# A decoder layer on one core: how the rounded tokens and the rounded FFN rows are turned

## Time and profile before

| what | us |
|---|---|
| median of 3 runs | 1321.93 (1319.57 to 1323.46) |
| the profiled execution | 1327.34 |
| its span, first to last instruction | 1325.5 |
| PE busy in the span | 1158.6 (87%) |
| DVE busy | 1048.7 (79%) |
| POOL busy | 951.8 (72%) |
| ACT busy | 866.6 (65%) |

### The profile page before, as it was taken

One profiled execution on the slowest core, in us unless ns is written; L12 is line 12 of the kernel. 1 busy time (PEld: TensorE's weight loads), 2 busy tenths in 40 slices (PEclk: granted clock), 3 DMA queues, 4 the chain that ended last, 5 costly groups with the idle time before them and its releaser, 6 DMA issues. The chain is left out here.

```text
span 1325.5 us, 33417 instructions
## 1 busy us (share of the span) xinstructions
PE 1158.6 (87%) x10082; PEld 828.7 (63%) x10082; DVE 1048.7 (79%) x3192; ACT 866.6 (65%) x1789; POOL 951.8 (72%) x1016
## 2 busy tenths in 40 slices
PE   4779998979989799899776699999999999999985
PEld 3566676757767576677543456666666666666652
DVE  5478886878868788788658688888888889888872
ACT  3467776767767677677756356666666666666664
POOL 0166675756756666667674499999999999999982
PEclk9879999998999999999886699999999999999997
DMA  5244654553445544454537244433334444444400
GB/s 193 73 152 139 199 174 159 175 174 119 142 160 174 167 135 147 145 174 154 167 134 281 90 137 120 126 124 124 131 132 130 131 132 135 135 135 135 127 25 24
DMA packets 87840, 186.57 MB, mean 141 GB/s; under 512 B 12176, under 2 KB 28816, under 8 KB 87760
## 3 DMA queue, kind: packets, MB, share of 16 engines
q1 hardware_dynamic: 86896, 185.02, 43.9%
q10 hardware_dynamic: 864, 0.66, 0.2%
HBM read 105.86 MB, written 54.61 MB: 121 GB/s over the span
## 5 line engine op out<-in xcount | busy, mean ns | idle before, releaser
L608 ACT ACTIVATE prob<-masked,negmax 128x128 f32<-128x128 f32 (+1 forms) x512 | 205.8, 452 | 129.7 <-DVE negmax L741 128.7
L741 DVE CUSTOM_DVE_ANT_0 masked<-s_ps,mask_f 128x128 f32<-128x128 f32 (+1 forms) x512 | 161.2, 352 | 43.4 <-issue 30.7
L988 PE MATMUL y_ps<-kv,toep 128*128 128x288 f16 x640 | 184.7, 289 | 1.4 <-DVE prod L1324 1.4
L990 PE MATMUL y_ps<-kv,toep 128*128 128x288 f16 x640 | 184.5, 288 | 0.0
L989 PE MATMUL y_ps<-kv,toep 128*128 128x288 f16 x640 | 184.5, 288 | 0.0
L1044 PE MATMUL f_ps<-w1T,xiT 128*128 128x512 bf16 (+1 forms) x768 | 174.7, 364 | 0.9 <-ACT xiT L1165 0.7
L1223 POOL TENSOR_TENSOR tree<-prod 128x512 f32<-128x512 f32 x128 | 163.2, 1275 | 1.2 <-DVE prod L1324 1.2
L386 POOL TENSOR_TENSOR kv_s<-kv_f,kv_s 128x1152 f16<-128x1152 f32 x64 | 154.5, 2415 | 11.4 <-ACT kv_s L622 11.3
L1172 ACT ACTIVATE silu<-gate,sx 128x512 f32<-128x512 f32 (+1 forms) x96 | 66.0, 687 | 139.6 <-DVE gate L1378 139.6
L747 DVE TENSOR_TENSOR pT_lo<-t_ps,pT_hi 128x384 f16<-128x384 f32 x256 | 140.8, 550 | 17.0 <-ACT pT_hi L616 16.5
L616 ACT CAST pT_hi<-t_ps 128x384 f16<-128x384 f32 x256 | 122.0, 477 | 41.6 <-PE t_ps L510 39.5
(11 more groups left out here) (154 smaller groups left out, 3540.3 us busy)
## 6 DMA issues: line engine op xcount, KB each, us to landing
kv_pairs<-kv_s SPq DMA_DIRECT2D x64, 576.0 KB, 4.0
kv<-kv_pairs SPq DMA_DIRECT2D x32, 1152.0 KB, 8.1
c_in<-in_ctxr SPq DMA_DIRECT2D x64, 192.0 KB, 3.5
x_in<-in_x SPq DMA_DIRECT2D x16, 512.0 KB, 6.1
q_st<-q_hi SPq DMA_DIRECT2D x128, 64.0 KB, 2.0
k_st<-k_hi SPq DMA_DIRECT2D x128, 64.0 KB, 2.0
x_res<-in_x SPq DMA_DIRECT2D x16, 512.0 KB, 5.1
x_after_attention<-x_out SPq DMA_DIRECT2D x16, 512.0 KB, 3.3
```

Source lines behind the costliest of these rows:

```text
L608: ins = nc.scalar.activation(prob[h % 2][:, at:at + w], masked[h % 2][:, at:at + w], ACT.Exp, bias=negmax[:, h % 2, t:t + 1], scale=-1.0)
L741: ins = nc.vector.tensor_tensor_reduce(masked[h % 2][:, at:at + w], s_ps[h % 2][:, at:at + w], mask_f[:, S - w:S], -1.0, FAR, ALU.add, ALU ...
L988: nc.tensor.matmul(dst, toep[p][:, 0, taps], c[:, 0, m], start=mt == 0, stop=False)
L990: mm = nc.tensor.matmul(dst, toep[p][:, 1, taps], c[:, 0, m], start=False, stop=mt == lt)
```

## The change

The two turns are done by DMA. SP issues `dma_start_transpose` from SBUF to SBUF: one for the 128 x 512 tokens, three for the 128 x 1408 hidden rows (chunks of 512, 512 and 384 columns). The PE transposes, the PSUM tile b_ps and the two ACT copies go. In SP's order of a round, the three hidden transposes of head r-3 stand ahead of `load_conv`, and the token transpose of head r-1 stands last, behind the two stores of y_out. `xiT_done` and `hiT_done` now count DMA completions (16 each). The down projection takes its blocks in the order 0 to 10 where it took 8, 9, 10, 0 to 7, still as a group of three and a group of eight; its first group now waits for all three chunks.

```diff
+            def turn_hidden(h):
+                for c, (at, w) in enumerate(CH):
+                    counts = (h * 3 + c + 1, h)
+                    for count in counts:
+                        if not isinstance(count, int):
+                            sp.lower_val(count)
+                    alone(sp, started)
+                    sp.wait_ge(hi_done, counts[0])
+                    if c == 0:
+                        reached(sp, d_full, counts[1])
+                    sp.dma_start_transpose(hiT[:, at // P:(at + w) // P, :], hid_i[:, at:at + w]).then_inc(hiT_done, 16)
+            def turn_tokens(h):
+                counts = (h + 1, h * 6)
...
+                alone(sp, started)
+                sp.wait_ge(xi_done, counts[0])
+                reached(sp, f_full, counts[1])
+                sp.dma_start_transpose(xiT[:], x_i[:]).then_inc(xiT_done, 16)
             def body(r, p, loop=False):
+                if live(r - 3, loop):
+                    turn_hidden(r - 3)
                 if live(r + 1, loop):
                     load_conv(sp, r + 1, 1 - p)
...
                     sp.wait_ge(out_done, r - 2)
                     for half in range(2):
                         sp.dma_start(tokens(out, r - 3, half), y_out[half * 64:half * 64 + 64, :]).then_inc(out_stored, 16)
+                if live(r - 1, loop):
+                    turn_tokens(r - 1)
```

```diff
             def gate_up(h, c, sides=(0, 1)):
                 at, w = CH[c]
                 if c == 0 and sides[0] == 0:
-                    pe.wait_ge(xiT_done, h + 1)
+                    pe.wait_ge(xiT_done, 16 * (h + 1))
...
-                    if c == 0 and side == 1:
-                        reached(pe, hiT_done, h * 2 - 1)
...
             def project_down(h, part):
-                pe.wait_ge(hiT_done, h * 2 + part + 1)
...
                 if part == 0:
-
+                    pe.wait_ge(hiT_done, 48 * (h + 1))
```

More of the change, by code:

```diff
@@ L860, in mixer @@
         sem(n) for n in ("xc_done", "amax_done", "vmax_done", "vrec_done", "sx_done", "xmul_done", "xt_done", "xi_done"))
-    xi_full, xiT_done = sem("xi_full"), sem("xiT_done")
+    xiT_done = sem("xiT_done")
     f_full, gate_done, silu_done, up_done, hid_done = (sem(n) for n in ("f_full", "gate_done", "silu_done", "up_done", "hid_done"))
@@ L864, in mixer @@
         sem(n) for n in ("hmax3_done", "hmax_done", "sh_done", "shr_done", "shi_done"))
-    ht_done, hi_done, hi_full, hiT_done = sem("ht_done"), sem("hi_done"), sem("hi_full"), sem("hiT_done")
+    ht_done, hi_done, hiT_done = sem("ht_done"), sem("hi_done"), sem("hiT_done")
     d_full, down_done, out_done, out_stored = sem("d_full"), sem("down_done"), sem("out_done"), sem("out_stored")
@@ L936, in mixer @@
     a_ps = ps("a_ps", [P, 512], F32)
-    b_ps = ps("b_ps", [P, 1024], BF16)
-    TURN = [(f_ps[1][:].bitcast(BF16), 8, IT - 8), (b_ps[:], 0, 8)]
     def rounds(eng, body):
@@ L1010, in mixed @@
                 mm.then_inc(yt_full, 1)
[L1012 to L1032, removed]
             def gate_up(h, c, sides=(0, 1)):
@@ L1046, in gate_up @@
                     mm.then_inc(f_full, 1)
+            PARTS = ((0, 3), (3, IT - 3))
             def project_down(h, part):
-                pe.wait_ge(hiT_done, h * 2 + part + 1)
-                t0, n = TURN[part][1:]
+                t0, n = PARTS[part]
                 if part == 0:
+                    pe.wait_ge(hiT_done, 48 * (h + 1))
                     pe.wait_ge(x2_done, min(h + 3, NH) if isinstance(h, int) else h + 3)
@@ L1055, in project_down @@
                 for t in range(t0, t0 + n):
-                    mm = nc.tensor.matmul(a_ps[:], hiT[:, t, :], w2T[:, t, :], start=t == TURN[0][1], stop=t == 7)
+                    mm = nc.tensor.matmul(a_ps[:], hiT[:, t, :], w2T[:, t, :], start=t == 0, stop=t == IT - 1)
                 if part == 1:
@@ L1069, in body @@
                     conv(r, p, 1)
-                if down_live:
-                    hidden_turned(r - 3, 0)
-                    hidden_turned(r - 3, 1)
                 if live(r - 1, loop):
@@ L1091, in body @@
                     conv(r, p, 3, (0,))
-                if live(r - 1, loop):
-                    tokens_turned(r - 1)
                 if conv_live:
@@ L1117, in round_tokens @@
                 act.wait_ge(xt_done, h + 1)
-                reached(act, xi_full, h)
+                reached(act, xiT_done, 16 * h)
                 nc.scalar.activation(x_i[:], x_t[:], ACT.Copy, bias=-MAGIC).then_inc(xi_done, 1)
@@ L1133, in whole @@
                     act.wait_ge(ht_done, h * 3 + c + 1)
-                    reached(act, hi_full, h * 2 - 1 if c == 2 else h * 2)
+                    reached(act, hiT_done, 48 * h)
                     nc.scalar.activation(hid_i[:, at:at + w], hid_t[:, at:at + w], ACT.Copy, bias=-MAGIC).then_inc(hi_done, 1)
@@ L1143, in round_hidden @@
                 whole(2)
[L1145 to L1150, removed]
             def queries_out(h, p):
@@ L1160, in queries_out @@
                 ins.then_inc(qt_done, 1)
[L1162 to L1165, removed]
             def silus(h, p, c):
@@ L1184, in body @@
                 ffn_live = live(r - 2, loop)
-                if live(r - 3, loop):
-                    hidden_out(r - 3, 0)
-                    hidden_out(r - 3, 1)
                 if ffn_live:
@@ L1201, in body @@
                     queries_out(r + 1, 1 - p)
-                if live(r - 1, loop):
-                    tokens_out(r - 1)
                 if ffn_live:
```

## The result

The changed kernel takes 1402.2 us (median of 4 runs, 1399.55 to 1404.68) beside 1320.95 us for the kernel before: a ratio of 1.0612 with a 95% interval of 1.0582 to 1.0643. Forecast were 1420 us, 1350 to 1530, slower. The 81.3 us lie in the last stage: from the first to the last of the 32 y_out the profiled executions take 519.0 us before (801.47 to 1320.48) and 600.5 after (792.88 to 1393.39), 81.5 more. The first 27 intervals between y_out give 74.2 of these (2.75 a round), the last four 7.3. The steady intervals were 17.02 in the mean; now five of the 27 are 18.8 to 18.9 and the others about 20.0 (a sixth short one, 18.6, follows them). The stretch ahead of the first y_out, nearly all of it unchanged code, happens to be 8.6 us longer in the profile of the kernel before; over the profiles of this case the first y_out ends between 792 and 803 us.

What follows compares the result with a forecast made beforehand. POOL's back-to-back 17.07 us round was taken as the bound. A late token transpose adds 3.1 us over 28 rounds (87), ends 8.5, 1.8 and 1: 98 on 1327.3 gives 1425, 1420 as median; range 1350 to 1530.

Steps and rivals of the forecast that it cites:

- G: Start of gate_up chunk 0 on PE, forecast at T+5.2 when the token transpose lands; break-even T+3.1.
- T: End of y_out on POOL, which raises `out_done`; the zero point for the times in a round.
- hand-over to `first_norm`: From gate_up's start through matmuls, gate and aggregate to POOL's `first_norm`, claimed to take 2.05 us.
- the low clock adds: PE's clock drops behind most gaps ahead of gate_up, lengthening the round from 19.2 to 20.2 us.
- Removal worth nothing, loads behind covered: PE's 0.92 us a round becomes a yT wait; toep and kv, issued later, keep six us of slack.
- The cover: Slack between the last hidden transpose landing, about T+8, and project_down at T+9.9: claimed 2 us.
- The round is POOL's: Last stage before the change: POOL's back-to-back 17.07 us sets the round, PE second, 0.5 us behind.
- Serial transposes: Rival: DMA transposes run one after another, project_down becomes late, 8.3 us more a round, 1570 us; chance 0.15.
- Full clock throughout: Rival: same stall ahead of gate_up but PE keeps 2.4 GHz, 2.1 us a round, 1392 us; chance 0.14.
- second case: Full-clock rival with the token landing at its lower bound as well: 0.8 us a round, 1351 us; chance 0.12.
- d: Landing of the token transpose, counted from y_out's end: T+5.2 forecast, bounds T+3.7 and T+7.1.
- PE's relief as a gain: Rival: the token transpose lands early and the period follows PE, 28 us less, 1294 us; chance 0.02.

Runs made afterwards that it cites:

- e1: The changed kernel with the token transpose moved ahead of the wait for y_out and both stores: 1324.4 us, ratio 1.0024 against the kernel before.
- e2: The changed kernel with the token transpose placed between the two stores of y_out: 1346.7 us, ratio 1.0185 against the kernel before.
- e10: The changed kernel with the tokens transposed twice, first into a spare tile nobody reads, then into xiT: 1441.9 us, ratio 1.0926.
- e4: The changed kernel with only the tokens turned by DMA, the hidden rows by PE and ACT as before: 1416.7 us, ratio 1.0719.
- e5: The kernel before with the addition that makes y_out moved from POOL to DVE: 1320.4 us, ratio 0.9987.
- e6: The changed kernel with the addition that makes y_out moved from POOL to DVE: 1327.0 us, ratio 1.0033.
- e8: The changed kernel with y_out's addition on DVE and the token transpose ahead of the stores: 1327.2 us, ratio 1.0051.
- e11: The kernel before without the last addition, so the stores take `down` and the last residual is left out: 1319.3 us, ratio 0.9986.
- e7: The changed kernel with 12 unread matmuls ahead of gate_up to keep PE busy in its gap: 1378.1 us, ratio 1.0414.

## Why the prediction was right

**Right.** The token transpose is late behind the stores, the aggregate hands the lateness to POOL, and the round becomes G plus a constant. e1, e2 and e10 move G by SP's order alone and the round follows. The steps as measured against the forecast:

| step | forecast | measured |
|---|---|---|
| transpose issued | T+2.1 | T+1.92 |
| issue to landing | 3.1 | 2.9 |
| G | T+5.2 | T+5.14 |
| hand-over to `first_norm` | G+2.05 | G+1.80 |
| `var` to the next T | 11.93 | 11.84 |
| round at full clock | 19.2 | 18.8 |
| the low clock adds | 1.0 | 1.2 |
| steady rounds in all | 87 | 74 |
| ends | 11 | 7 |

Steady rounds are 28 in the forecast and the first 27 intervals in the measurement.

The landing agrees with the rule of the Trainium skill (Advanced Engine Details and Errata, X-Bar Transpose) that transposing DMAs are about as fast as plain ones: 128 KB in 2.9 us stand between the 2.0 for 64 KB and 3.5 for 192 KB of the earlier trace rows.

**Removal worth nothing, loads behind covered.** Both right: PE's relief became a yT wait (e1), and kv is never awaited. e4 adds a condition: under the stall and the low clock the relief is worth something.

**Too dear by 17 us (98 against 81.5).** What the sum adds to G was 0.34 us too long at full clock, mostly the hand-over: forecast were 1.03 for the matmuls, 0.67, 0.17 and 0.18, but gate starts at 1058.09 = G+0.94, no hand-over behind the matmuls' modelled end. Over the rounds that is most of the 13 us. The clock's term came out near its size by two errors against each other: it was charged to every round, 28 us, where five of 27 kept the upper level and the others lost 1.2 us each, some 26. The ends were 4 us less.

**SP's price for a transpose was mis-sized.** Forecast 0.7 us, as for a store. The rows of SP's issues in the kernel after (count, and ns lowest/median/highest):

```profile
L977 SPq DMA_TRANSPOSE xiT<-x_i x23: 1237/1251/1255, 856.6 to 1290.3; - x23
L966 SPq DMA_TRANSPOSE hiT<-hid_i x69: 1177/1188/1204, 858.1 to 1294.4; - x69
```

So toep and kv are issued at T+7.5 and T+8.2 instead of T+5.4. The issue of the last hidden transpose begins near 1058.1, and it lands 2.4 us behind that, near 1060.5; project_down begins at 1061.59. The cover was 1.1 us, not 2. In e2, where G is 1.4 us earlier, it is used up.

**The bound.** "The round is POOL's" was half right. POOL's order and the loop of three engines had the same length within 0.1 us. For this change it made no difference, since either gives no gain for PE's relief; for e5, e6, e8 and e11 it did, and their expectations missed by it.

**The rivals.** *Serial transposes* is refuted: 4 blocks land in 2.9 us, three transposes of 3 to 4 blocks issued 1.3 us apart land 2.4 us after their issue each, and e10's doubled one costs an issue, not a landing. The estimate of 1309 ns a block in a row from the Trainium skill (VectorE: DVE Perf Modes, The three transpose paths) falls with it: by that estimate 4 blocks in a row take 5.2 us, and they land in 2.9. *Full clock throughout* was true of five of the 27 rounds, and e7 made it true of all: 1378 where that rival had 1392. (Its second case takes d = 3.9, although the prediction's own lower bound of the landing is T+3.7; with that it would be some 5 us less.) *PE's relief as a gain* is refuted by e1, where the transpose lands in time and the time doesn't fall.

## What to carry to other kernels

A DMA that feeds the next step goes ahead of any wait and store on its queue that does not feed it: two lines of SP's order were worth 78 us here, and the transposes themselves nothing in a steady round. An engine with no idle time need not be the only bound: follow the waits of the second engine through a whole round and see whether they close a loop, before work is taken off the first. A stall of TensorE has to be priced twice, once for the lateness and once for the clock behind it, here some 57 and 24 us.

## What the runs showed of the hardware

- The issue of a transpose from SBUF to SBUF holds SP for 1.18 to 1.25 us, beside 0.77 for each of two stores of y_out in a row (0.67 to 0.69 for a store by itself in e2) and 0.40 for toep.
- Gaps of nearly the same length had either outcome for TensorE's clock. In the kernel after it stayed at 1.00 behind waits of 2.78, 2.79, 2.82 and 2.83 us and fell behind 2.77 and 2.81; the other waits of its first 27 rounds, up to 3.58 us, were followed by 0.66 to 0.71 over the next 5 us. In e4 it fell behind waits of 2.51 to 2.72 us in every steady round but one (2.55), and in e2 it stayed up behind 1.34 to 1.88.
- A DVE add of two f32 SBUF tiles and a POOL add held each other off, 0.73 to 1.26 us on POOL and 0.69 to 1.27 on DVE. The Trainium skill states such a lock (SBUF — State Buffer, Who interferes with whom), and these rows agree: who began first went at its usual pace.
- 65,500 more small packets, the transposes', slowed neither of the two loads beside them whose landing the profile gives: kv took 7.5 us from issue to landing, 8.1 before, and toep 4.4 in the steady rounds, 4.8 before.
